# A routed feed-forward kernel on one core: PSUM banks and buffers between the up and the down products are dealt out anew

## The reference

```python
x = x + 0.5 * ffn(layernorm(x))
x = x + mixer(layernorm(x))
x = x + 0.5 * ffn(layernorm(x))

def ffn(x):                                   # 12 experts, each token goes to 3
    topw, sel = top_k(x @ Wg, 3)              # softmax over the three gives cw
    h = gelu(x @ Wup[e] + bup[e])             # 128 -> 512
    y = h @ Wdown[e] + bdown[e]               # 512 -> 128
    return sum over e of cw[e] * y
```

## Time and profile before

| | us |
|---|---|
| timed runs, median of 3 | 641.77 (635.78 to 642.45) |
| span of the profiled execution | 966.7 |
| TensorE busy in it | 657.6 |
| ScalarE | 415.2 |
| GpSimd | 413.2 |
| VectorE | 346.1 |
| granted TensorE clock, mean | 0.798 |

### The profile page before, as it was taken

One profiled execution on the slowest core, in us unless ns is written; L12 is line 12 of the kernel. 1 busy time (PEld: TensorE's weight loads), 2 busy tenths in 40 slices (PEclk: granted clock), 3 DMA queues, 4 the chain that ended last, 5 costly groups with the idle time before them and its releaser, 6 DMA issues.

```text
span 966.7 us, 17693 instructions
## 1 busy us (share of the span) xinstructions
PE 657.6 (68%) x4591; PEld 600.8 (62%) x4591; DVE 346.1 (36%) x1636; ACT 415.2 (43%) x1280; POOL 413.2 (43%) x432
## 2 busy tenths in 40 slices
PE   7566888734962199966777114999656677788863
PEld 6465887723961089855676104988546576788851
DVE  6811242401100058854330103789323314212224
ACT  2533454401630068744343102888333245545433
POOL 1336545573057600054433772000444435666664
PEclk9578888855985589987777556999778788989986
DMA  7634444542662255533354233744242455766616
GB/s 213 169 111 121 128 136 134 153 113 72 171 180 61 57 158 144 153 108 98 94 143 142 65 84 87 207 138 141 74 123 85 132 157 135 215 179 171 172 39 228
DMA packets 121843, 127.87 MB, mean 132 GB/s; under 512 B 17178, under 2 KB 84561, under 8 KB 121749
## 3 DMA queue, kind: packets, MB, share of 16 engines
q1 hardware_dynamic: 106452, 99.52, 35.8%
q0 software_dynamic: 12992, 26.11, 9.7%
q10 hardware_dynamic: 2304, 1.11, 0.4%
HBM read 96.62 MB, written 30.79 MB: 132 GB/s over the span
## 4 chain that ended last, share of the span: by engine, by line
PE 45%; another core or an unknown queue 30%; DVE 7%; issue 7%; ACT 4%; SPq 2%; POOL 1%; DMA 1%; ACTq 1%; DVEq 0%; POOLq 0%
PE ps L860 18%; PE ps L873 17%; ACT hT L1024 3%; PE ps L830 2%; PE ps L729 2%; PE ps L755 1%; POOL YG L671 1%; PE ps L821 1%; DVE Ys L1556 1%; DVE YG L1487 1%; PE ps L802 1%; SPq L520 1%; PE ps L803 1%; ACTq L1024 1%
## 5 line engine op out<-in xcount | busy, mean ns | idle before, releaser
L1024 ACT ACTIVATE hT<-ps,BU 128x128 f32<-128x128 f32 x944 | 267.4, 375 | 398.2 <-remote 249.5
L860 PE MATMUL ps<-xT,WU 128*128 128x128 f32 x1888 | 293.4, 302 | 138.1 <-issue 82.4
L860 PEld LDWEIGHTS ps<-xT,WU 128*128 128x128 f32 x1888 | 265.8, 215 | 158.7 <-issue 156.6
L873 PE MATMUL ps<-WD,hT 128*128 x1888 | 283.4, 296 | 93.2 <-issue 64.8
L873 PEld LDWEIGHTS ps<-WD,hT 128*128 128x128 f32 x1888 | 258.3, 211 | 102.7 <-issue 102.5
L1556 DVE TENSOR_TENSOR Ys<-ps,BD 128x128 f32<-128x128 f32 x236 | 66.8, 289 | 554.9 <-remote 357.1
L658 POOL DMA_INDIRECT xs<-XN,SX x144 | 143.2, 994 | 280.9 <-issue 164.2
L671 POOL DMA_INDIRECT YG<-ys,SY x144 | 146.4, 1017 | 113.8 <-DMA ys<-Ys 70.9
L645 POOL DMA_INDIRECT xl<-xn,SG x59 | 59.9, 1015 | 80.2 <-PE ps L830 39.6
L680 POOL DMA_INDIRECT yk<-Ys,row x59 | 59.1, 1001 | 47.4 <-DVE Ys L1556 36.5
L1001 ACT ACTIVATE xT<-ps 128x512 f32<-128x512 f32 (+1 forms) x55 | 32.7, 595 | 61.2 <-remote 49.4
(11 more groups left out here) (255 smaller groups left out, 532.3 us busy)
## 6 DMA issues: line engine op xcount, KB each, us to landing
WU<-in_L_ffn_Wup_dram SPq DMA_DIRECT2D x236, 256.0 KB
ys<-Ys SPq DMA_DIRECT2D x42, 256.0 KB
xl<-xs SPq DMA_DIRECT2D x118, 66.0 KB
xl<-xs SPq DMA_DIRECT2D x59, 64.0 KB
WD<-in_L_ffn_Wdown_dram SPq DMA_DIRECT2D x12, 256.0 KB, 5.0
WD<-yk SPq DMA_DIRECT2D x4, 768.0 KB, 4.7
xs<-XN,SX POOLq DMA_INDIRECT x144
YG<-ys,SY POOLq DMA_INDIRECT x144
```

Source lines behind the costliest of these rows:

```text
L860: x = e.matmul(HB[i % 2][:, c * P:(c + 1) * P], WU[i % NW][:, c * P:(c + 1) * P], xT[m % 2][:, j * P:(j + 1) * P], start=True, stop=True)
L873: x = e.matmul(YB[i % 2][:, 0:D], hT[i % 3][:, c * P:(c + 1) * P], WDf[:, bass.ds(r + c * P, P)], start=(c == 0), stop=(c == C - 1))
L1024: x = e.activation(hT[i % 3][:, c * P:(c + 1) * P], HB[i % 2][:, c * P:(c + 1) * P], ACT.Gelu, bias=BU[:, bass.ds(b + c, 1)])
```

## The change

Three banks `HB` for up products and two `YB` banks with two tiles each (columns 0 to 127 and 128 to 255), so one bank less for the transposes and side steps. Down products come three tiles behind the up products, not two. There are five `hT` buffers. VectorE waits for the second down product of a pair and then adds the bias of both; a down product that begins a pair waits until both tiles of the pair two before are read. `ring` deals out three banks, with 3.5 slots for the readers of step A3. SyncE stores each group two slots later, and ScalarE's two stores of a pass's last group come after the GELUs of tiles 2 and 3. GpSimd's list is unchanged.

```diff
+LAG = 3
+NHB = 3
+NHT = 5
+BANK = NHB + 2
+NSIDE = 8 - BANK
-READ = {("A2", 1): 2, ("A3", 0): 3, ("A5", 1): 2}
+READ = {("A2", 1): 2, ("A3", 0): 3.5, ("A5", 1): 2}
 def downs(i):
-    return [i - 2, i - 1, i] if i == NI - 1 else [i - 2] if i >= 2 else []
+    return list(range(i - LAG, NI)) if i == NI - 1 else [i - LAG] if i >= LAG else []
+def pair(i):
+    n, _, k = TILES[i]
+    return (NTL + 1) // 2 * n + k // 2
+def pair_end(j):
+    n, x = j // ((NTL + 1) // 2), j % ((NTL + 1) // 2)
+    return NTL * n + min(2 * x + 2, NTL)
...
-    free, now, n = [0] * 4, -1, 0
+    free, now, n = [0] * NSIDE, -1, 0
...
-            b = min(range(4), key=lambda x: (free[x], (x - n) % 4))
-            used.setdefault(step, []).append((4 + b, last.get(b)))
+            b = min(range(NSIDE), key=lambda x: (free[x], (x - n) % NSIDE))
+            used.setdefault(step, []).append((BANK + b, last.get(b)))
...
-        HB, YB = psum[0:2], psum[2:4]
+        HB, YB = psum[0:NHB], psum[NHB:NHB + 2]
-        hT = [sb(f"hT{i}", [P, HID]) for i in range(3)]
+        hT = [sb(f"hT{i}", [P, HID]) for i in range(NHT)]
...
-                if n < 3 and k % 4 == 2 and k >= 4:
+                if n < 3 and k % 4 == 0 and k >= 8:
+                    store_y(m - 2)
+                if n < 3 and k == NTL - 1:
                     store_y(m - 1)
...
-                if i >= 2:
-                    e.wait_ge(s_h, i - 1)
+                if i >= NHB:
+                    e.wait_ge(s_h, i - NHB + 1)
...
-                if i >= 2:
-                    e.wait_ge(s_Y, i - 1)
+                if k % 2 == 0 and pair(i) >= 2:
+                    e.wait_ge(s_Y, pair_end(pair(i) - 2))
                 for c in range(C):
-                    x = e.matmul(YB[i % 2][:, 0:D], hT[i % 3][:, c * P:(c + 1) * P], WDf[:, bass.ds(r + c * P, P)],
+                    x = e.matmul(YB[pair(i) % 2][:, k % 2 * D:k % 2 * D + D], hT[i % NHT][:, c * P:(c + 1) * P], WDf[:, bass.ds(r + c * P, P)],
...
-                if i >= 3:
-                    e.wait_ge(s_dn, i - 2)
+                if i >= NHT:
+                    e.wait_ge(s_dn, i - NHT + 1)
...
-                if k < 2 and n:
+                if 2 <= k < 4 and n:
...
-                    e.wait_ge(s_Y, NTL * n - 1 + k)
+                    e.wait_ge(s_Y, NTL * n - 3 + k)
...
             def bias_down(i):
                 n, h, k = TILES[i]
-                e.wait_ge(s_dn, i + 1)
+                e.wait_ge(s_dn, pair_end(pair(i)))
...
                 for x in downs(i):
-                    bias_down(x)
+                    if x + 1 == pair_end(pair(x)):
+                        for y in range(x - TILES[x][2] % 2, x + 1):
+                            bias_down(y)
```

More of the change, by code:

```diff
@@ L856, in up @@
                 e.wait_ge(*((s_xh, m - n - 1) if k >= singles(n) else (s_xh0, single(n, k) + 1)))
-                if i >= 2:
-                    e.wait_ge(s_h, i - 1)
+                if i >= NHB:
+                    e.wait_ge(s_h, i - NHB + 1)
                 for c in range(C):
-                    x = e.matmul(HB[i % 2][:, c * P:(c + 1) * P], WU[i % NW][:, c * P:(c + 1) * P],
+                    x = e.matmul(HB[i % NHB][:, c * P:(c + 1) * P], WU[i % NW][:, c * P:(c + 1) * P],
                                  xT[m % 2][:, j * P:(j + 1) * P], start=True, stop=True)
@@ L901, in _ @@
                 e.wait_ge(*drained(LAST[x]))
-                e.matmul(psum[4 + x][:], ident[:], X[:, 4 * g:4 * g + 4, :].rearrange("p t d -> p (t d)"),
+                e.matmul(psum[BANK + x][:], ident[:], X[:, 4 * g:4 * g + 4, :].rearrange("p t d -> p (t d)"),
                          start=True, stop=False)
@@ L905, in _ @@
                     e.wait_ge(s_fs, K * x + k + 1)
-                    i = e.matmul(psum[4 + x][:].rearrange("p (t d) -> p t d", d=D), ident[:], YL[:, 4 * q:4 * q + 4, k, :],
+                    i = e.matmul(psum[BANK + x][:].rearrange("p (t d) -> p t d", d=D), ident[:], YL[:, 4 * q:4 * q + 4, k, :],
                                  start=False, stop=(k == K - 1))
@@ L1020, in gelu @@
                 e.wait_ge(s_up, i + 1)
-                if i >= 3:
-                    e.wait_ge(s_dn, i - 2)
+                if i >= NHT:
+                    e.wait_ge(s_dn, i - NHT + 1)
                 for c in range(C):
-                    x = e.activation(hT[i % 3][:, c * P:(c + 1) * P], HB[i % 2][:, c * P:(c + 1) * P], ACT.Gelu,
+                    x = e.activation(hT[i % NHT][:, c * P:(c + 1) * P], HB[i % NHB][:, c * P:(c + 1) * P], ACT.Gelu,
                                      bias=BU[:, bass.ds(b + c, 1)])
@@ L1041, in _ @@
                 gelu(i)
-                if k < 2 and n:
+                if 2 <= k < 4 and n:
                     m = NG * n - 1
-                    a, b = (0, size(NG - 1) - 1) if k == 0 else (size(NG - 1) - 1, size(NG - 1))
-                    e.wait_ge(s_Y, NTL * n - 1 + k)
+                    a, b = (0, size(NG - 1) - 1) if k == 2 else (size(NG - 1) - 1, size(NG - 1))
+                    e.wait_ge(s_Y, NTL * n - 3 + k)
                     e.dma_start(ys[(n - 1) % 2].rearrange("(j p) d -> p j d", p=P)[:, 4 * (NG - 1) + a:4 * (NG - 1) + b, :],
@@ L1064, in _ @@
                 e.wait_ge(s_fp, x + 1)
-                e.activation(X[:, 4 * g:4 * g + 4, :].rearrange("p t d -> p (t d)"), psum[4 + x][:], ACT.Copy
+                e.activation(X[:, 4 * g:4 * g + 4, :].rearrange("p t d -> p (t d)"), psum[BANK + x][:], ACT.Copy
                              ).then_inc(s_fe, 1)
@@ L1555, in bias_down @@
                     e.wait_ge(*stored(m - NYS))
-                e.tensor_tensor(Ys[m % NYS][:, k % 4, :], YB[i % 2][:, 0:D], BD[:, bass.ds(bd_at.pop((m, k % 4)), D)],
+                e.tensor_tensor(Ys[m % NYS][:, k % 4, :], YB[pair(i) % 2][:, k % 2 * D:k % 2 * D + D], BD[:, bass.ds(bd_at.pop((m, k % 4)), D)],
                                 ALU.add).then_inc(s_Y, 1)
```

## The result

The changed kernel takes 648.52 us (median of 4 runs), the kernel before beside it 640.89: 1.011 times as long, 95% interval 1.006 to 1.017. The forecast was 632 us.

A forecast was written before the change was run, and what follows sets the result against it. The unrecorded kernel was taken to be near two bounds, TensorE's work (590 us) and GpSimd's transfers (584). From 641.8, 13 us of relief, plus 2 for side banks and 1 for queue order, gave 632; range 618 to 653.

The forecast's parts named there:

- the relief of 13 us in the sum: TensorE's waits for up and down banks: time saved, taken between 6 us (a seventh) and 44 us (all).
- The signs that were to prove it right: Profile after: up and down waits from 46 and 28 us to under 15 each, clean stretches unchanged, passes one and four shorter.
- the order in the queues: Stores, loads and gathers queued behind later Y results: cost between 0 and 11 us, taken at 1.
- sign for being wrong: Profile after, ends of passes: GpSimd's waits for the last store grow by 3 us at each pass.
- The rival: Ends of the passes: later last stores delay GpSimd's gathers, 3 x 3.6 = 11 us, slower at 652 us; chance 0.20.
- GpSimd's 584 of the 642 us: GpSimd's 406 transfers and gaps, 530 us, with at most 44 ahead and 10 behind: 58 less than the median.
- The three side banks: Banks shared by transposes and mixing chain, three instead of four: cost between 0 and 12 us, taken at 2.
- The tail: Very end: one more down, perhaps two scatters and a gather left over, 3.9 us or 0; taken at 0.
- the sum of 517: TensorE's work in the four passes: 4434 records at 0.11, 488 us, plus about 29 for wide ones.
- the 52 us of idle time: TensorE's time without work in the median run: 641.8 less 590 us of work, start and end.
- the rival of no change: Late starts are the recorder's doing, or GpSimd's 530 us set the pace: 642 us; chance 0.30.
- The rival from the Trainium skill: Within the no-change case (0.30): late starts may be waits for instructions, which mostly hidden fetching would make vanish unrecorded.

The follow-up runs named there:

- the inner part alone: Changed kernel with each pass's last down products and stores timed as before; three up banks, pairs, three side banks remain: 642.65 us, ratio 1.002; 940.95 where the old takes 953.6.
- The two stores alone: Kernel before with only ScalarE's two last-group stores moved after the GELUs of tiles 2 and 3: 650.23 us, ratio 1.017; later 967.27 and 955.26 in long executions.
- the side-by-side runs: Changed kernel and kernel before with only the late stores, on one chip: 952.06 and 943.37 us against 967.27 and 955.26.

## Why the prediction was wrong

**The step that failed** is the relief of 13 us in the sum, "nearer to the lower end, because the long gaps of the record clearly vanish". It was worked out from waits of 46.4 and 28.1 us of a record whose length was half as much again as the timed runs. I scaled what I found there, to a seventh and then up to 13. In an execution of the kind that is timed the wait for GELUs is 1.9 us and nothing is relieved: the inner part alone measures 1.002. What to ask was not how much of these waits is real, but whether the places in which the recorded execution was 325 us too long are the same in which the waits stood. They were: in the stretches of the earlier trace rows, without GpSimd's transfers, TensorE is busy for 79 of 80 us, and the length was lost elsewhere. Where the kernel takes 953 us the inner part is worth 12.7 us, so the mechanism exists there. That 12.7 is close to the 13 of the sum is luck: the 13 was chosen for the 642 us kernel, and for the recorded one the prediction had up to 44. The signs that were to prove it right could not have told either: in the changed kernel both waits are under 15 us, but so they are in the kernel before at 639 us.

**The term that was mis-sized** is that of the order in the queues: between 0 and 11 us, taken at 1. The two stores alone cost 11.3 us (650.2 against 638.9), the upper end. With it the prediction's sign for being wrong came true: in the changed kernel the waits for the last stores grew by 4.7, 1.3 and 2.4 us, 2.8 on average where 3 was named. The rival named the mechanism, the place and 652 us, and got 0.20. Against it I had that GpSimd's scatters begin some 20 tiles before a pass ends, 62 us of them, and would still run. They do, but only just: in the kernel before's own profile the scatters of the second pass run from 272.4 to 334.3, and the last store is issued at 328.2. At the first end the same store took 4.5 us to land; by that (an estimate) 1.6 us are left here, less than the two tiles' 3.6. I should have set the two ends against each other; what a delay has beyond the time that is left goes into the chain.

**What was right.** GpSimd's 584 of the 642 us: in the profile of the kernel before its transfers take 535 us, with 39.6 ahead of them and 9.0 behind. The holes of 27.8 and 25.2 us before the scatters and the 2.5 at the last end are the rest. The three side banks: taken at 2 us, measured 1.0 with an interval from 0 to 3. The tail: taken at nothing, and in the changed kernel's profile GpSimd's last pass is 141.3 us of transfers without a hole, as in the kernel before (141.9). That TensorE stands near its own bound beside it: in the changed kernel's four passes it is busy for 532 of 560 us. It stands nearer to it than the sum of 517 had it: in the kernel before's passes it is busy for 530 of 555 us. So the 52 us of idle time, which had to be somewhere and spoke against the rival of no change, were 25 in the passes; the rest was work and a longer last stretch.

**The rival from the Trainium skill** (Runtime: NRT & Kernel Launch, section on instruction fetch, which says that fetching is mostly hidden) would have the late starts vanish, and where the kernel takes 640 us they do. Elsewhere they stay, with 204 to 288 us on ScalarE. The record of 966.7 us speaks against waits for instructions as their cause. Two of the longest late starts:

```profile
320.09 1.15 ACT L1024 ACTIVATE hT<-ps,BU 128x128 f32<-128x128 f32 x4 [29.12 <-remote]
...
338.99 0.29 DVE L1556 TENSOR_TENSOR Ys<-ps,BD 128x128 f32<-128x128 f32 x1 [37.54 <-remote]
```

And all the queues that moved anything between 296 and 343 us:

```profile
q0 software_dynamic: 992, 2.03, 17.7%
q1 hardware_dynamic: 315, 0.35, 2.1%
```

The two queues that carry instructions are not among them, so neither start was released by a block of instructions that had just come. For the other late starts this was not looked at.

**What stays open.** The changed kernel lost 7.6 us and the late stores alone 11.3, but their intervals (1.006 to 1.017 and 1.014 to 1.020) overlap, and the side-by-side runs fell where the kernel before takes over 950 us. The holes at the ends differ by half a microsecond only (11.44 and 11.96). With the stores a tile earlier 3.5 us of loss have no hole that accounts for them. The stores alone and the inner part alone (1.2 us) add up to 12.5 us, the whole change lost 7.6. No version beat the kernel before at 640 us.

## What to carry to other kernels

Look first whether the recorded execution is of the kind that is timed. Here the spans of the right kind lay about 2 us under their timed length, and that of the wrong kind 325 us above the timed runs; its waits belonged to another case, and scaling them didn't help. Where one engine's list is a chain of transfers back to back, follow each thing it waits for at its ends; a store that is moved by two tiles to suit a deeper pipeline elsewhere cost 9 to 11 us at three ends, about the two tiles each time, although no busy engine does more. A deeper pipeline should be emptied where another engine waits for its last results (the inner part with the old ends costs 1 us or nothing). In this case it paid only in the executions whose profiles show that its buffers are waited for.

## What the runs showed of the hardware

The kernel before took 636 to 645 us in two groups of more than twenty runs and 946 to 967 in three others, each group on a chip of its own. It is not only the chip: among the 25 runs of one group of the first kind stand a single one of 965.4 and one of 731.9 us.

In the long executions GpSimd's transfers have the same pitch (1.30 us from one to the next), and a GELU instruction takes as long (375 ns in the record of 966.7 us, 372 in the one of 639.1), as does a bias add (289 ns in both). What is added is that, while GpSimd issues transfers, the other engines start late. ScalarE does so by 204 to 288 us in all and VectorE by 310 to 361 with no releaser on record. TensorE does it too: its loads of up weights stood 156.6 us with nothing on record to wait for, against 14.0 in the short execution, and within one up product single matmul records came 2.1 us apart, where the eight of an up product in the earlier trace rows take 1.06 in all:

```profile
330.48 0.37 PE L860 MATMUL ps<-xT,WU 128*128 128x128 f32 x1 [1.73 <-issue]
...
332.58 0.37 PE L860 MATMUL ps<-xT,WU 128*128 128x128 f32 x1 [1.73 <-issue]
```

So the holds hit all engines at once, which the prediction named as a way to be wrong. During the 48 gathers of the second and third pass, which last 62 to 64 us in both, the recorded execution of 966.7 us starts the GELUs of four tiles, the one of 639.1 those of 26 to 29. The second pass's gathers, in the columns of the earlier trace rows, in the long and then in the short execution:

```profile
272.40:334.70 62.30, 17.71 (x92) 14.58 (x90) 0.88 (x3) 5.18 (x17) 47.91 (x48) 0.57 0.31 86
```
```profile
180.80:244.60 63.80, 63.51 (x532) 60.30 (x533) 41.02 (x173) 50.27 (x152) 49.48 (x48) 1.00 0.81 234
```

The granted clock of TensorE is 0.57 of full speed on average where TensorE was busy for 17.7 of 62.3 us, and 1.00 where it was busy for 63.5 of 63.8. The cause of the late starts isn't shown.
